# Expert rows fetched and added batch by batch inside the attention that follows, its first context loaded ahead of the expert weights, and the 64 wide attention unrolled

## The chip, the cores and the metric

The kernel runs as one program on one core of a Trainium2 chip. Its time is the device time of one execution in microseconds. The kernel before took 2455.58 us (median of three runs, 2454.81 to 2457.07). A core has five engines with instruction streams of their own: TensorE (PE: matmuls and transposes, with weight loads shown as PEld), VectorE (DVE), ScalarE (ACT), GpSimd (POOL) and SyncE (SP), which here only issues transfers. Engines meet through semaphores: an instruction adds to one when it is done, another engine waits for a value. Each stream is in order, so what stands behind a waiting instruction waits too.

## The reference

An input x (8 batches, 256 rows, 256 columns, float32) goes through eight gated branches, each `x = x + tanh(gate) * branch(layernorm(x))`, with a context of 8 x 256 x 192:

- layer 0: a cosine similarity with the context, then a feed-forward with one expert;
- layer 1: attention of 16 heads of width 16 on the context (l1x), then a mixture of 8 experts of 682 hidden columns, of which each row uses the two with the largest gate (l1f);
- layer 2: attention of 16 heads of width 64 on the context (l2x), then a mixture of 8 experts of 256 hidden columns, top 2, and two shared experts (l2f);
- layer 3: attention of 16 heads of width 16 on the context (l3x), then a self attention of width 16 with register rows (l3f).

```python
# layer 1 and 2, the mixtures, cut
top_v, top_i = top_k(gate_logits, 2)
out[row] = sum over the two chosen experts e of gate[row, e] * W3[e] @ (silu(W1[e] @ x[row]) * (W2[e] @ x[row]))
```

## The kernel before

x lies in SBUF through all branches as `x[128, 16, 256]`: 16 tiles of 128 rows, two tiles (T = 2) to each of the B = 8 batches. The branches run one after the other. At the end of each, DVE adds one to the semaphore `phase`, and the engines that touch shared buffers wait for it before they go on.

**Mixtures (l1f, l2f).** The 2048 rows are sorted by expert through a table in DRAM, `rows_by_expert`. POOL writes every row twice into it, at the slots of its two experts (line 835, an indirect DMA with the slots in `sli`). For 23 blocks of 256 rows, SP loads the block, PE transposes it and runs the up and down matmuls with weights split in high and low parts, ACT copies the result out, and SP stores it in place in the table (line 561, semaphores `ys0` to `ys3`). When every block has been stored, POOL fetches the rows back: for each of the 16 tiles two indirect DMAs of 128 rows (lines 851 to 855), 32 in all, into `r.back`, which lies over the arena from its start. DVE waits for eight at a time and then adds `gw * row` to x, two `scalar_tensor_tensor` instructions per tile, each followed by a wait for itself (lines 1390 to 1394). Only then does it raise `phase` (line 1398). `ch.link` is this wait of DVE for its own last instruction.

**The 64 wide attention (l2x)** follows l1f. For each batch n: DVE takes the mean and variance (`statistics`), POOL the power -0.5 (`root`, line 719), DVE writes the normed rows (`front`), PE transposes them, ACT copies them to `xt`. PE projects queries and keys (line 1877) and values (line 1890), which needs `xt`, the context `ct` and the weights. For each of 16 heads: scores (line 1900), maximum on DVE (line 1053), exponential on ACT (line 1555), on POOL one over the sum (line 889) and the multiplication by it (line 893), transposes on PE (line 1913), a copy on DVE (line 1062), values on PE (line 1928). After the heads, PE multiplies by the output weights (line 1958) and DVE adds to x (`finish`, lines 1075 and 954). The order is written out by hand: the statistics of batch n + 1 stand on DVE in the heads of batch n, after the copy of head 0 (`h == LAG`, line 1063), and its `root` stands on POOL after the multiplication of head 0 (line 895), before that of head 1. Batches 0 to 6 are one hardware loop on DVE, ACT, PE and POOL (`Fori(0, B - 1)`), batch 7 is written out behind it. SP loads contexts in `contexts` (line 491). Ahead of that, it issues ten transfers with the weights of the first five experts of l2f (`first_experts`, line 520), which wait for the same `phase` as the attention; they share its queue.

**The attention of l3x** follows l2f and is written out batch by batch. Its program (`packing`, one function on each engine) runs from n = -3 to B: in step n, PE makes the scores of batch n + 1 (line 2051, with the maxima on DVE, line 1133), those of batch n transposed (line 2065, exponential on ACT, line 1625, `clamp` on POOL, line 780) and its values (line 2085), and projects queries, keys and values of batch n + 3 (lines 1774 to 1776). POOL splits contexts (`context`), normed rows (`xT`), queries (`qhl`) and keys (`khl`) into two parts each (lines 750 and 752), adds a bias to x (line 773) and does the root. SP moves the split queries and keys into packed tiles (line 582). Before step -3, POOL sets three `kpack` tiles (line 738), a tile `qx` (lines 740 and 745) and does the root of batch 0; `with_bias(0)` comes last.

Of the kernel before, what the change touches and what calls it, by code (L numbers as in the profile page):

```python
# [13 lines left out]
F32 = mybir.dt.float32  # L14
# [8 lines left out]
P = 128  # L23
# [93 lines left out]
class Mix:  # L117
# [4 lines left out]
    def __init__(self, name, f, ring, cuts, slots, shared):  # L122
# [11 lines left out]
        self.total = {"lg": B, "gd": 1, "ga": 1, "rk": 1, "mk": 1, "sl": 1, "dy": 1, "sc": 16 * 2 * NT,  # L134
# [5 lines left out]
        for q in range(4):  # L140
            self.total[f"gt{q}"] = 16 * 2 * NT // 4
# [81 lines left out]
def build(nc, a, out, layers=8):  # L223
    ctx = ExitStack()
    with ctx:
# [42 lines left out]
        with ExitStack() as packed:  # L268
# [5 lines left out]
            oT16 = lay("oT16", [P, 4, S], F32)  # L274
            wqs16 = lay("wqs16", [P, 2, DC, D])
# [102 lines left out]
        for s in (L1F, L2F):  # L378
# [11 lines left out]
            r.back = arena[:, 0:2 * NT * D].rearrange("p (t d) -> p t d", d=D)  # L390
# [52 lines left out]
        mo = group("mo", "lg", "gd", "ga", "rk", "mk", "sl", "dy", "sc", "gt0", "gt1", "gt2", "gt3",  # L443
# [40 lines left out]
        def _(sp):  # L484
# [6 lines left out]
            def contexts(name, sem_in, sem_used, per):  # L491
# [151 lines left out]
        def _(pool):  # L643
# [89 lines left out]
            def packing(s):  # L733
                m, at = pk, s.base
                pool.wait_ge(g["phase"], n_phase[s.name] - 1)
                if not s.own:
                    for b in range(3):
                        nc.gpsimd.memset(kpack[b][:, :, :].bitcast(F32), 1.0).then_inc(m["ones"], 1)
                if s is L3X:
                    nc.gpsimd.memset(qx[:, :].bitcast(F32), 0.0).then_inc(m["qi"], 1)  # L740
                    pool.wait_ge(m["qi"], 1)
                    for j in range(2):
# [4 lines left out]
                        pool.wait_ge(m["qi"], 2 + j)  # L747

# [63 lines left out]
            def mixture(s):  # L812
# [38 lines left out]
                for t in range(NT):  # L851
                    for w in range(2):
                        nc.gpsimd.indirect_dma_start(  # L853
                            r.back[:, 2 * t + w, :], None, all_rows,
                            bass.IndirectOffsetOnAxis(ap=sli[:, w, t:t + 1], axis=0)).then_inc(m[f"gt{t // 4}"], 16)
                if not s.shared:
                    for dst, src in later:
                        pool.dma_start(dst, src).then_inc(g["w3_in"], 16)

            for name in run:  # L860
# [21 lines left out]
                else:  # L882
# [1511 lines left out]
```

## Time and profile before

| what | value |
|---|---|
| median of three runs | 2455.58 us |
| the profiled execution | 2458.67 us |
| its span in the trace | 2456.9 us |
| PE busy | 1932.6 us, 79% |
| DVE busy | 1015.9 us, 41% |
| ACT busy | 732.9 us, 30% |
| POOL busy | 999.5 us, 41% |
| granted TensorE clock, mean | 0.854 of 2.4 GHz |

Times in the trace count from the start of the span. A "busy" engine is one that executes an instruction other than a wait, a branch or the issue of a transfer; for POOL the issue of an indirect DMA is counted. The profile follows the chain of work that ended last back from the end; its shares say what lay on the path. A row of a timeline gives the start, the duration and in brackets the idle time of that engine before it, with what ended it. The stages lie in the span about so: l1f from 483 to 953 us, l2x to 1583, l2f to 1883, l3x to 2122.

### The profile page before, as it was taken

The page shows a single profiled execution, that of the slowest core. Times are in us where ns is not written, and L with a number is a line of the kernel's source. Part 1 is how long each engine was busy: PE and PEld are TensorE (multiplying, and loading weights), DVE is VectorE, ACT ScalarE, POOL GpSimd, SP SyncE. Part 2 cuts the span into 40 slices and gives each one's busy share as a digit, 9 for nine tenths or more (in the row PEclk, how much of TensorE's full clock was granted, in tenths as well). Part 3 has the DMA queues.
Part 4 walks back from the last instruction along what each step waited for, and adds up shares of the span by engine and source line. Part 5 has one row for each costly group of instructions (what it writes and reads, how often), then busy time and mean ns, then how long its engine had stood idle before and what let it go on. Part 6 is the DMA issues. An engine that isn't in the chain of part 4 may idle for free.

```text
span 2456.9 us, 33526 instructions
## 1 busy us (share of the span) xinstructions
PE 1932.6 (79%) x11738; PEld 1465.6 (60%) x11738; DVE 1015.9 (41%) x2339; ACT 732.9 (30%) x1721; POOL 999.5 (41%) x1044
## 2 busy tenths in 40 slices
PE   3589599727999962898988989769981899647997
PEld 2477466426888852555655656569970666435664
DVE  2434478531222212433334323543223578443773
ACT  1122056302222210332333323312330355312564
POOL 4010443064666643432344323461666676303320
PEclk9799789558999985888988989879995689766999
DMA  4270446114565543000000000012752645004441
GB/s 141 96 259 0 61 75 99 56 65 149 186 200 187 199 149 124 4 3 3 3 0 3 3 3 0 1 54 65 248 165 68 88 67 76 2 0 67 77 72 40
DMA packets 123393, 194.15 MB, mean 79 GB/s; under 512 B 12128, under 2 KB 99168, under 8 KB 122560
## 3 DMA queue, kind: packets, MB, share of 16 engines
q1 hardware_dynamic: 94288, 144.84, 24.6%
q0 software_dynamic: 8480, 26.65, 3.4%
q10 hardware_dynamic: 20496, 20.97, 2.6%
q8 instruction: 77, 1.26, 0.2%
q14 instruction: 52, 0.43, 0.1%
HBM read 109.84 MB, written 43.52 MB: 62 GB/s over the span
## 4 chain that ended last, share of the span: by engine, by line
PE 61%; issue 15%; POOL 9%; DVE 8%; DMA 3%; SPq 2%; ACT 2%; DVEq 0%; POOLq 0%; ACTq 0%
PE bank L2264 8%; PE bank L1774 6%; PE bank L2051 5%; PE bank L1900 5%; PE bank L1775 5%; PE bank L1776 5%; PE bank L1877 5%; PE bank L2085 3%; PE bank L1913 3%; PE bank L1928 3%; POOL arena L853 2%; PE bank L1890 2%; DVE nmf L1133 2%; SPq L582 1%; POOL rows_by_expert L835 1%
## 5 line engine op out<-in xcount | busy, mean ns | idle before, releaser
L1133 DVE TENSOR_REDUCE nmf<-bank 128x2 f32<-128x512 f32 x384 | 257.4, 688 | 144.8 <-PE bank L2051 142.9
L1625 ACT ACTIVATE pT<-bank 128x512 f32<-128x512 f32 x384 | 225.5, 595 | 224.2 <-PE bank L2065 222.7
L1774 PE MATMUL bank<-split,ewl 128*128 128x256 f32 x818 | 245.3, 300 | 9.6 <-DVE split L1361 9.6
L1371 DVE TENSOR_TENSOR arena<-sil,bank 128x256 f32<-128x256 f32 x216 | 91.1, 422 | 358.9 <-ACT sil L1709 358.8
L1776 PE MATMUL bank<-split,ewh 128*128 128x256 f32 x818 | 233.2, 285 | 0.0
L1775 PE MATMUL bank<-split,ewh 128*128 128x256 f32 x818 | 233.1, 285 | 0.0
L2051 PE MATMUL bank<-kpack,qpack 48*128 48x256 f32 (+1 forms) x768 | 199.6, 361 | 33.1 <-DVE nmf L1133 18.9
L889 POOL TENSOR_TENSOR esum<-esum,minus 128x2 f32<-128x2 f32 x128 | 89.2, 697 | 324.4 <-ACT arena L1555 324.2
L1489 ACT ACTIVATE arena<-bank 128x512 f32<-128x512 f32 x162 | 96.7, 597 | 388.4 <-PE bank L2264 158.5
L2264 PE MATMUL bank<-ew,arena 128*128 128x256 f32 (+1 forms) x864 | 210.2, 389 | 2.1 <-issue 2.1
L823 POOL TENSOR_TENSOR ewl<-ew,ewh 128x1536 fp32r<-128x1536 f32 (+1 forms) x71 | 206.9, 2914 | 5.7
L2065 PE MATMUL bank<-qpack,kpack 50*128 50x256 f32 (+1 forms) x768 | 192.8, 351 | 4.4 <-ACT pT L1625 4.1
L2051 PEld LDWEIGHTS bank<-kpack,qpack 48*128 48x128 f32 (+1 forms) x768 | 125.0, 213 | 118.6 <-DVE nmf L1133 57.1
L1555 ACT ACTIVATE arena<-bank,nmax 128x256 f32<-128x256 f32 x256 | 118.7, 469 | 244.1 <-DVE nmax L1053 242.1
L1053 DVE TENSOR_REDUCE nmax<-bank 128x2 f32<-128x512 f32 x128 | 87.6, 690 | 230.1 <-PE bank L1900 226.9
L2264 PEld LDWEIGHTS bank<-ew,arena 128*128 128x128 f32 (+1 forms) x864 | 155.2, 190 | 41.9 <-issue 25.3
L821 POOL CAST ewh<-ew 128x1536 fp32r<-128x1536 f32 (+1 forms) x71 | 88.4, 1245 | 212.4 <-DMA ew<-in_we 201.5
L1774 PEld LDWEIGHTS bank<-split,ewl 128*128 128x128 f32 x818 | 158.3, 194 | 18.4 <-issue 17.7
L1775 PEld LDWEIGHTS bank<-split,ewh 128*128 128x128 f32 x818 | 158.5, 194 | 0.8
L1900 PE MATMUL bank<-arena 64*128 64x256 f32 x512 | 154.0, 443 | 6.2 <-ACT arena L1489 6.2
L1776 PEld LDWEIGHTS bank<-split,ewh 128*128 128x128 f32 x818 | 158.3, 194 | 0.0
L1709 ACT ACTIVATE sil<-bank 128x256 f32<-128x256 f32 x216 | 82.7, 383 | 233.9 <-PE bank L1776 233.9
(403 smaller groups left out, 3844.1 us busy)
## 6 DMA issues: line engine op xcount, KB each, us to landing
ew<-in_we SPq DMA_DIRECT2D x46, 768.0 KB, 4.5
rows_by_expert<-mrow ACTq DMA_DIRECT2D x1, 20480.0 KB, 62.8
qpack<-qhl SPq DMA_DIRECT2D x144, 128.0 KB
kpack<-khl SPq DMA_DIRECT2D x144, 128.0 KB
ew<-in_we SPq DMA_DIRECT2D x23, 640.0 KB, 5.5
ew<-in_we SPq DMA_DIRECT2D x25, 512.0 KB, 4.4
arena<-rows_by_expert SPq DMA_DIRECT2D x46, 256.0 KB, 3.8
rows_by_expert<-arena SPq DMA_DIRECT2D x46, 256.0 KB, 4.1
```

Of the source, the lines that this page charges most:

```text
L823: nc.gpsimd.tensor_tensor(low, whole, high, ALU.subtract).then_inc(m["ws"], 1)
L1133: V.tensor_reduce(nmf[:, c, :, j, r], bank[h % 2][:, :].rearrange("p (t k) -> p t k", t=T), AXX, ALU.max, negate=True).then_inc(m["mx"], 1)
L1555: ins = A(prob[h % 3][:, t * S:(t + 1) * S], bank[h % 3][:, t * S:(t + 1) * S], ACT.Exp, bias=nmax[:, h, t:t + 1], accum_out=esum[:, h, t: ...
L1625: A(pT16[i % 8][:, :], bank[2 + h % 2][:, :], ACT.Exp, scale=s.qscale).then_inc(m["e"], 1)
L1774: mm(out_, al, bh, start=start, stop=False)
L1775: mm(out_, ah, bl, start=False, stop=False)
L1776: return mm(out_, ah, bh, start=False, stop=stop)
L1877: ins = mm(dst, w[:, c, gr * P:(gr + 1) * P], of[:, c, :], start=c == 0, stop=c == kt_ - 1)
L1900: ins = mm(bank[h % 3][:, t * S:(t + 1) * S], qT[r0:r0 + 64, gr, t * P:(t + 1) * P], kT[r0:r0 + 64, gr, :], start=True, stop=True)
L2051: ins = mm(bank[h % 2][:, t * S:(t + 1) * S], q[rows, r, t * P:(t + 1) * P], k[rows, r, :], start=True, stop=True)
L2065: ins = mm(bank[2 + h % 2][:, t * S:(t + 1) * S], k[rows, r, t * P:(t + 1) * P], q[rows, r, :], start=True, stop=True)
L2264: ins = mm(bank[4 + k % 2][:, q * D:(q + 1) * D], r.hid[(s.a0[k] + n) % s.slots][rr, q * P:(q + 1) * P], expert_down(s, w)[rr, h, :], star ...
```

## The change

1. The 32 indirect fetches and the additions leave the end of both mixtures. POOL's part ends when every block is stored, DVE waits for the same (`ys0` to `ys3`) and raises `phase`.
2. A new function `gather(s, n)` on POOL issues the four indirect DMAs of batch n, into one of three buffers. A new function `add_rows(ch, s, n)` on DVE waits for these four, does the four additions with two links (tile 0 and 1 of the first expert, link, tile 0 and 1 of the second, link), and adds one to `ga`; the fetch of batch n from n = 3 on waits for the additions of batch n - 3.
3. In l2x POOL issues the fetches of batches 0 and 1 before its first root, and those of batch n + 2 after the last head of batch n. DVE adds batch 0 before `statistics(0)`, batch n + 1 at `h == LAG` in the heads of batch n, directly before `statistics(n + 1)`.
4. In l3x POOL sets `qx` first, then issues the fetches of batches 0 and 1, then sets the `kpack` tiles; the fetch of batch n + 5 stands at the head of step n (n = -3 to 2), before `context`. DVE adds batch 0 before `statistics(0)` and batch n + 4 at `h == 8` of step n.
5. SP issues the first context of l2x ahead of the ten transfers of expert weights.
6. The loops over batches 0 to 6 of l2x are written out on DVE, ACT, PE and POOL.
7. The three transfers of l3x weights (`later`) go from the end of l1f to the end of l2x on POOL, since the fetch buffers of l1f lie over their target.

```diff
@@ SP
                 sp.dma_start(ct[:, :, :], a["ctxT"][0, :, :, :]).then_inc(sem_in, 16)
+                if sets:
+                    first_experts(sets, a["we2"])
...
-            if "l2f" in run:
-                first_experts(L2F, a["we2"])
             if "l2x" in run:
-                contexts("l2x", ph["l2x"]["ct"], ph["l2x"]["v"], L2X.vjobs)
+                contexts("l2x", ph["l2x"]["ct"], ph["l2x"]["v"], L2X.vjobs, L2F if "l2f" in run else None)
@@ POOL, packing
                 pool.wait_ge(g["phase"], n_phase[s.name] - 1)
-                if not s.own:
-                    for b in range(3):
-                        nc.gpsimd.memset(kpack[b][:, :, :].bitcast(F32), 1.0).then_inc(m["ones"], 1)
                 if s is L3X:
...
+                    for n in range(2):
+                        gather(L2F, n)
+                if not s.own:
+                    for b in range(3):
+                        nc.gpsimd.memset(kpack[b][:, :, :].bitcast(F32), 1.0).then_inc(m["ones"], 1)
...
                     ahead = 0 <= n + 3 < B
+                    if s is L3X and 2 <= n + 5 < B:
+                        gather(L2F, n + 5)
@@ POOL, mixture
                     pool.wait_ge(m[f"ys{q}"], at[f"ys{q}"] + s.total[f"ys{q}"])
-                for t in range(NT):
+
+            all_rows = table.rearrange("b s d -> (b s) d")
+
+            def gather(s, n):
+
+                m, at = mo, s.base
+                if n >= 3:
+                    pool.wait_ge(m["ga"], at["ga"] + n - 2)
+                for t in range(T):
                     for w in range(2):
                         nc.gpsimd.indirect_dma_start(
-                            r.back[:, 2 * t + w, :], None, all_rows,
-                            bass.IndirectOffsetOnAxis(ap=sli[:, w, t:t + 1], axis=0)).then_inc(m[f"gt{t // 4}"], 16)
-                if not s.shared:
-                    for dst, src in later:
-                        pool.dma_start(dst, src).then_inc(g["w3_in"], 16)
+                            rooms[s.name].back[n % 3][:, w, t, :], None, all_rows,
+                            bass.IndirectOffsetOnAxis(ap=sli[:, w, n * T + t:n * T + t + 1], axis=0))\
+                            .then_inc(m[f"gt{n % 3}"], 16)
@@ POOL, l2x
+                    gather(L1F, 0)
+                    gather(L1F, 1)
                     root(m, 1, rstd[:, :], rstd[:, :], mhalf[:, 0:T])
-                    with pool.Fori(0, B - 1) as n:
-                        normalise(n, True)
-                    normalise(B - 1, False)
+                    for n in range(B):
+                        normalise(n, n < B - 1)
+                        if n + 2 < B:
+                            gather(L1F, n + 2)
+                    pool.wait_ge(mo["ga"], L1F.base["ga"] + B)
+                    for dst, src in later:
+                        pool.dma_start(dst, src).then_inc(g["w3_in"], 16)
@@ DVE
+            def add_rows(ch, s, n):
+
+                m, at = mo, s.base
+                dve.wait_ge(m[f"gt{n % 3}"], at[f"gt{n % 3}"] + 16 * 2 * T * (n // 3 + 1))
+                for w in range(2):
+                    for t in range(T):
+                        r = n * T + t
+                        ins = stt(x[:, r, :], rooms[s.name].back[n % 3][:, w, t, :], gw[:, w, r:r + 1], x[:, r, :],
+                                  ALU.mult, ALU.add)
+                    ch.link(ins)
+                V.memset(idle[:, 0:1], 0.0).then_inc(m["ga"], 1)
...
                         if h == LAG and ahead:
+                            add_rows(ch, L1F, n + 1)
                             statistics(n + 1)
...
+                add_rows(ch, L1F, 0)
                 statistics(0)
...
-                with dve.Fori(0, B - 1) as n:
-                    ch.loop(n, 2 * T + LN)
+                for n in range(B - 1):
                     heads(n, True)
                     projected(n + 1)
                     heads(n + 1, False, range(LAG))
                     finish(n)
-                ch.leave(B - 1)
@@ DVE, packing
+                    if s is L3X:
+                        add_rows(ch, L2F, 0)
                     statistics(0)
...
+                        if h == 8 and n + 4 < B and s is L3X:
+                            add_rows(ch, L2F, n + 4)
                         if h == 10 and n + 4 < B and not s.own:
                             statistics(n + 4)
@@ DVE, mixture
-                for t in range(NT):
-                    if t % 4 == 0:
-                        dve.wait_ge(m[f"gt{t // 4}"], at[f"gt{t // 4}"] + 16 * 8)
-                    for w in range(2):
-                        ch.link(stt(x[:, t, :], r.back[:, 2 * t + w, :], gw[:, w, t:t + 1], x[:, t, :], ALU.mult, ALU.add))
+                for q in range(4):
+                    dve.wait_ge(m[f"ys{q}"], at[f"ys{q}"] + s.total[f"ys{q}"])
@@ ACT and PE, l2x
-                with act.Fori(0, B - 1) as n:
+                for n in range(B - 1):
...
-                with pe.Fori(0, B - 1) as n:
+                for n in range(B - 1):
```

## Rows read from the trace of the kernel before

**Rows 1.** The page, the chain that ended last: shares by engine.
```profile
PE 61%; issue 15%; POOL 9%; DVE 8%; DMA 3%; SPq 2%; ACT 2%; DVEq 0%; POOLq 0%; ACTq 0%
```
**Rows 2.** The chain in order of time, 903 to 984 us: start, us, what.
```profile
903.55 2.13 DMA rows_by_expert<-arena
...
906.61 1.03 POOL arena L853
...
946.37 2.72 DMA arena<-rows_by_expert,sli
...
958.47 8.97 DMA ct<-in_ctxT
...
967.57 15.69 PE bank L1877 x64
```
**Rows 3.** Timelines of POOL, DVE and ACT, 915 to 958 us.
```profile
915.52 0.96 POOL L853 DMA_INDIRECT arena<-rows_by_expert,sli  x1 [0.31 <-issue]
...
918.29 4.17 DVE L1394 SCALAR_TENSOR_TENSOR x<-arena,gw,x 128x256 f32<-128x256 f32 x8 [21.65 <-DMA arena<-rows_by_expert,sli]
...
954.69 0.72 POOL L719 TENSOR_TENSOR rstd<-rstd,mhalf 128x2 f32<-128x2 f32 x1 [5.69 <-DVE rstd L1030]
...
957.45 0.60 ACT L1489 ACTIVATE xt<-bank 128x512 f32<-128x512 f32 x1 [54.07 <-PE bank L1860]
```
**Rows 4.** Timelines of POOL, PE and DVE in l2x: batch 1's heads, and batch 7's (last row).
```profile
1073.34 0.69 POOL L719 TENSOR_TENSOR rstd<-rstd,mhalf 128x2 f32<-128x2 f32 x1 [8.74 <-DVE rstd L1030]
...
1075.87 1.11 PE L1913 MATMUL bank<-ident,arena 128*128 128x128 f32 x4 [4.34 <-POOL arena L893]
...
1070.83 0.69 DVE L1053 TENSOR_REDUCE nmax<-bank 128x2 f32<-128x512 f32 x1 [0.52 <-DVE x L954]
...
1537.03 0.69 DVE L1053 TENSOR_REDUCE nmax<-bank 128x2 f32<-128x512 f32 x1 [0.20 <-DVE x L954]
```
**Rows 5.** Stretches, one per batch of l2x: us, busy (instructions) by engine, PE clock, DMA.
```profile
1272.51:1350.92 78.41, 69.52 (x308) 46.21 (x309) 27.62 (x49) 23.64 (x77) 28.22 (x33) 0.89 0.01 3
1350.92:1424.64 73.72, 64.82 (x308) 43.61 (x309) 27.34 (x49) 23.53 (x77) 28.12 (x33) 0.95 0.01 3
```
**Rows 6.** The chain in order of time, 1833 to 1901 us.
```profile
1833.95 2.13 DMA rows_by_expert<-arena
...
1883.68 5.32 POOL kpack L738 x3
...
1890.55 0.73 POOL rstd L719
...
1900.72 0.58 PE bank L1774
```
**Rows 7.** Timelines of POOL and PE, start of l3x.
```profile
1921.83 0.61 POOL L750 CAST khl<-kf 128x512 fp32r<-128x512 f32 x1 [0.82 <-DMA kpack<-khl]
...
1928.87 0.58 PE L1774 MATMUL bank<-xT,rows 128*128 128x256 f32 x1 [0.43 <-POOL xT L752]
```
**Rows 8.** POOL's clamp of head 3 and the values on PE, steps 0 and 2.
```profile
1944.99 0.61 POOL L750 CAST cT<-ct 96x512 fp32r<-96x512 f32 x1 [1.54 <-PE bank L1776]
...
1949.17 0.61 POOL L780 TENSOR_SCALAR pT<-pT 128x512 f32<-128x512 f32 x1 [0.48 <-ACT pT L1625]
...
2002.13 0.61 POOL L780 TENSOR_SCALAR pT<-pT 128x512 f32<-128x512 f32 x1 [0.36 <-ACT pT L1625]
...
1950.62 1.84 PE bank L2085 x16
...
2003.20 0.99 PE bank L2085 x16
```
**Rows 9.** DVE timeline in l3x: two instructions beside POOL, one with POOL idle.
```profile
1891.31 0.73 DVE L1128 TENSOR_SCALAR xn<-x,mv,rstd 128x256 f32<-128x256 f32 x2 [5.80 <-POOL rstd L719]
...
1907.33 1.95 DVE L1128 TENSOR_SCALAR xn<-x,mv,rstd 128x256 f32<-128x256 f32 x2 [10.42 <-POOL rstd L719]
...
2010.09 0.69 DVE L1133 TENSOR_REDUCE nmf<-bank 128x2 f32<-128x512 f32 x1 [0.48 <-PE bank L2051]
```

More of the change, by code:

```diff
@@ L133, in __init__ @@
         self.base = defaultdict(int)
-        self.total = {"lg": B, "gd": 1, "ga": 1, "rk": 1, "mk": 1, "sl": 1, "dy": 1, "sc": 16 * 2 * NT,
+        self.total = {"lg": B, "gd": 1, "gx": 1, "rk": 1, "mk": 1, "sl": 1, "dy": 1, "sc": 16 * 2 * NT,
                       "wh": self.parts * self.sets, "ws": self.parts * self.sets,
@@ L139, in __init__ @@
             self.total[n] = self.a0[-1]
-        for q in range(4):
-            self.total[f"gt{q}"] = 16 * 2 * NT // 4
+        self.total["ga"] = B
+        for q in range(3):
+            self.total[f"gt{q}"] = 16 * 2 * T * len(range(q, B, 3))
         for q in range(4):
@@ L274, in build @@
             oT16 = lay("oT16", [P, 4, S], F32)
+            with nc.sbuf_tensor("back16", [P, 3 * 2 * T * D], F32) as back16:
+                pass
             wqs16 = lay("wqs16", [P, 2, DC, D])
@@ L389, in build @@
             assert o[0] <= ARENA, (o[0], ARENA)
-            r.back = arena[:, 0:2 * NT * D].rearrange("p (t d) -> p t d", d=D)
+            r.back = [(back16 if s.shared else w13)[:, k * 2 * T * D:(k + 1) * 2 * T * D].rearrange("p (w t d) -> p w t d", w=2, t=T)
+                      for k in range(3)]
         assert o[0] <= ARENA, (o[0], ARENA)
@@ L442, in build @@
         l0f = group("l0f", "yc", "h", "hc", "y", "dve")
-        mo = group("mo", "lg", "gd", "ga", "rk", "mk", "sl", "dy", "sc", "gt0", "gt1", "gt2", "gt3",
+        mo = group("mo", "lg", "gd", "gx", "rk", "mk", "sl", "dy", "sc", "gt0", "gt1", "gt2", "ga",
                    "w0", "w1", "w2", "w3", "w4", "wd0", "wd1", "wd2", "wd3", "wd4", "wh", "ws", "xg0", "xg1", "xg2", "xg3",
@@ L489, in _, with contexts @@
                 sp.dma_start(dst, src).then_inc(g["w0_in"], 16)
-            def contexts(name, sem_in, sem_used, per):
+            def contexts(name, sem_in, sem_used, per, sets=None):
                 if n_phase[name] > 1:
@@ L1063, in heads @@
                         if h == LAG and ahead:
+                            add_rows(ch, L1F, n + 1)
                             statistics(n + 1)
-                        if isinstance(n, int) and n == B - 1 and 0 <= h - 4 < B - 1 and not steps_:
+                        if n == B - 1 and 0 <= h - 4 < B - 1 and not steps_:
                             stats_of(h - 4)
@@ L1275, in mixture @@
                 if s.shared:
-                    dve.wait_ge(m["ga"], at["ga"] + 1)
+                    dve.wait_ge(m["gx"], at["gx"] + 1)
                     ch.link(V.tensor_reduce(gm[:, :], sel[:, :, :], AXX, ALU.add))
@@ L1299, in mixture @@
                 if not s.shared:
-                    dve.wait_ge(m["ga"], at["ga"] + 1)
+                    dve.wait_ge(m["gx"], at["gx"] + 1)
                 ch.link(tt(sel[:, :, :], sel[:, :, :], lg[:, :, :], ALU.mult))
@@ L1557, in heads @@
                             ins.then_inc(m["e"], 1)
-                        if h == FRONT + 1 and not isinstance(n, int):
+                        if h == FRONT + 1 and n < B - 1:
                             front(n + 1)
@@ L1696, in mixture @@
                 act.wait_ge(m["gd"], at["gd"] + 1)
-                A(sel[:, :, :], sel[:, :, :], ACT.Exp).then_inc(m["ga"], 1)
+                A(sel[:, :, :], sel[:, :, :], ACT.Exp).then_inc(m["gx"], 1)
                 def high_part(k):
@@ L1878, in project @@
                             ins.then_inc(m[what], 1)
-                    if isinstance(n, int):
+                    if n == 0:
                         pe.wait_ge(g["w2b_in"], 16 * 2)
```

## The prediction

> **What bounds the kernel now.** I read the page's chain of waits first, then the same chain in order of time at the two places where a mixture ends, then the timelines of each engine there and in the stages behind it, and last the stretches of l2x. PE carries 61% of the chain [rows 1]; what matters is where it does not. At the end of l1f the table is stored at 905.7 us. POOL then issues 32 indirect DMAs, the first at 906.61, the last at 946.37, so one each 1.28 us; the last lands after 2.72 us [rows 2]. DVE adds in pace with them, eight additions in 4.17 us, 0.52 us each, the last eight done at 953.3 [rows 3]. Statistics follow; POOL's root starts at 954.69 and the transposed rows are in `xt` at 958.05 [rows 3]. But PE starts the projections only at 967.57, since the first context, issued at 958.47 behind ten weight transfers, takes 8.97 us to land [rows 2]. From the stored table to the first projection: 61.9 us. At the end of l2f the store lands at 1836.08; memsets of `kpack` start at 1883.68 and take 5.32 us, the root of batch 0 starts at 1890.55, the first projection at 1900.72 [rows 6]. Both stretches are latency with PE idle, so what leaves them is gained in full, and what is put on the chain of the next stage is paid in full.
>
> **Start of l2x.** The fetches of batches 0 and 1 stay ahead: the eighth starts at 915.52 as today, 1.27 us apiece, and ends at 916.48 [rows 3]; the root follows at about 916.7. DVE beside it: fetch 4 starts at 906.61 + 3 x 1.27 = 910.4, lands 2.72 us later at 913.1, four additions of 0.52 and 1.3 us of statistics (953.35 to 954.6) end at 916.5. Both paths meet at 916.7. From the root to `xt` it is 3.4 us (954.69 to 958.05) [rows 3], so the projections could start at 920.3, 47.3 us earlier. Against it: 3.9 MB of expert weights are now in flight at just that time. Today nothing runs beside the fetches; the nearest row is the context behind these weights, 8.97 us instead of 2.4 [rows 2]. A fetch has a queue of its own, so it need not wait for all of them. Its landing is bounded by 2.72 and by 8.97 us; I take twice 2.72 in round numbers, 2.9 us more. That leaves 44.4 us (bounds 41 and 47).
>
> The first context ahead of the weights is worth 9.4 us today (958.05 to 967.57, less the issue), but nothing in the new order: behind the weights it would be there 14 us after the phase (953.4 to 967.4), at about 920, before `xt` is. I count it within the 44.4 and not again.
>
> **Additions in l2x, seven times.** In batch n POOL has multiplied head 0 and stands in the root of batch n + 1, which waited 8.74 us for DVE's `rstd`; heads 1 and on stand behind it on POOL, and PE waits 4.34 us for them [rows 4]. So the statistics are on the chain in every batch, with nothing beside. The four additions stand directly before them: 4 x 0.52 = 2.1 us, seven times, +14.6 us. Bounds: 11 (two of a pair overlap a little) and 17. The fetches themselves (5.1 us a batch) start after POOL's last head, while PE projects and multiplies by the output weights; POOL is idle there for some 28 us, so they cost nothing; without this cover each batch would pay 5.1.
>
> **Unrolling.** At the head of each looped batch DVE loses 0.52 us before its first maximum where the unrolled batch 7 loses 0.20 [rows 4]. With about as much (0.17) on ACT at the tail of the batch, 7 x 0.49 = -3.4 us (bounds 0 and -6). The Trainium skill (Runtime: NRT & Kernel Launch, Instruction fetch mechanics) says that instructions stream in ahead in order and that a taken branch can force a fetch; by it each of seven back edges could hold such a fetch, and writing them out would bring more than I count. The trace shows only the 0.3 us, and the sum goes by that.
>
> **Clock.** After the wait of 4.34 us PE runs at 1.2 GHz, in most batches for some 13 us. A batch takes 78.41 us at a mean granted clock of 0.89, but 73.72 us where it came back earlier (0.95) [rows 5]. With a wait of 6.4 us I expect the slow kind to stay the rule. One batch more or less of either kind is 4.7 us: it goes into the range, at zero in the sum. The transfers of l3x weights at the end of l2x fall into POOL's idle time: zero.
>
> l2x together: -44.4 + 14.6 - 3.4 = **-33.2 us**.
>
> **Start of l3x.** The phase comes at about 1836.3. `qx` takes 1.6 us, eight fetches 10.2 (to 1848.4), `kpack` 5.3, the root starts at 1853.9 instead of 1890.55 [rows 6]: -36.7 us. DVE is there earlier (fetch 4 lands at 1845, additions and statistics end at 1848.6) and hides behind POOL. But then three times four fetches stand at the head of steps -3, -2 and -1, each 4 x 1.27 = 5.1 us, ahead of the context, of `xT`, `qhl` and `khl`. POOL is what the start of l3x waits for: the gaps between its work are 0.82 us (its `khl` waits for packed keys) and PE waits for its `xT` [rows 7]. So 3 x 5.1 - 0.8 = +14.4.
>
> **Fetches in steps 0, 1, 2.** There POOL's clamps of heads 0 to 3 must be done before PE's values. In step 0 POOL had 1.54 and 0.48 us to wait on the way and the clamp ended 0.84 us before PE came: 5.1 - 2.9 = 2.2 us. In step 2 it had 0.36 and ended 0.46 before: 5.1 - 0.8 = 4.3 [rows 8]. Step 1 I put between them, 3.2. Sum +9.7 (bounds 0 and 15.3).
>
> **Additions in steps -1 to 3** (those of -3 and -2 hide behind POOL). Four take 2.1 us alone. DVE has about 0.48 us of idle time before a maximum, and PE can run one head ahead [rows 9]. But DVE also suffers beside POOL: the same pair of instructions took 1.95 us beside POOL's work where it took 0.73 alone, 0.6 more for one [rows 9]. Four additions are thus between 2.1 and 4.5 us, less a slack of some 1 us: I take 2.0 for each step, five times, +10 (bounds 0 and 22). On this stands a rule of the Trainium skill (SBUF — State Buffer, "SBUF: two separate sides"): a DVE instruction with two inputs in SBUF and a GpSimd instruction exclude each other for their whole length. The long row agrees. By it the additions, with two such inputs, go at the upper end in l3x and at 2.1 in l2x, where POOL waits.
>
> l3x together: -36.7 + 14.4 + 9.7 + 10 = **-2.6 us**. l1f, l2f and all else are as before. Sum: **-35.8 us**. The profiled execution took 2458.67 us with a span of 2456.9, so 1.8 lie around the span and stay; it would be 2422.9. It stands 3.1 above the median of the runs; from the median 2455.58 the same difference gives **2420 us**.
>
> **Rivals.**
> 1. *The fetches and additions hide in l3x.* For it: DVE and POOL are not busy all the time there, and PE at 1.2 GHz leaves slack. Against it: rows 7 and 8 show POOL ahead of PE by less than a microsecond. Then l3x brings -36.7 + 14.4 + 4 = -18, l2x -36: 2401 us. 23%.
> 2. *POOL and DVE exclude each other fully in l3x*, the skill's rule above. The five additions go at 4.4 less nothing, +22, the fetches at +15.3: l3x -36.7 + 14.4 + 15.3 + 22 = +15; l2x with landings at 8.97 and 17 us of additions: -41 + 17 - 2 = -26: 2445 us. For it the long row [rows 9]; against it that DVE is not beside POOL at all times. 15%.
> 3. *Slower: the unrolled l2x has its instructions late.* A body of about 310 matmuls and as many weight loads is then fetched seven times by PE instead of once. It would take 36 / 7 = 5.1 us of stall in each batch to eat the gain, beyond that it is slower; at 6 us a batch 2462 us. Against it: batch 7 of l2x and all of l3x are written out already and show no such wait. 4%.
> 4. *It does not do what it says*: the attention waits for the last fetch after all, through POOL's order or one of the three buffers (`ga`). Then 32 fetches still stand before l2x and l3x; the context's 9.4 us, the unrolling's 3.4 and two additions of 2.1 are gained, 14.6 in l2x and some 2 in l3x are added: about 2455 us, no change. Against it: every wait on `ga` is for additions two steps back. 3%.
>
> **Numbers.** Forecast 2420 us, 55%, its own range 2408 to 2434. With rivals 1 and 2 the range is 2398 to 2440, which leaves out their far parts and rival 3. Two kernels closer than 0.2% (4.9 us) can't be told apart here. Faster by more than that: 0.93; within it: 0.03, rival 4; slower: 0.04, rival 3.
>
> **What would show it.** The first `xt` projection of l2x 15 to 19 us after the last store of l1f; if it is at 25, the weights slow the fetches. PE's wait before head 1 at 6.4 us in seven batches; if it stays at 4.3, the additions are hidden. Batches of l2x at 80 us. The root of batch 0 of l3x 17.8 us after the store, the first values of l3x (1950.62 now) about 20 us earlier, and its last ones only about 3. DVE's additions longer than 0.52 us in l3x and not in l2x. The prediction is wrong if l3x as a whole gains over 12 or loses over 10 us, or if the batches of l2x come out under 77 us.

## The result, and the profile after

The changed kernel took 2391.14 us (median of 4, 2380.09 to 2392.55), the kernel before beside it 2455.19 us (median of 4): a ratio of 0.9731, 95% interval 0.970 to 0.9763. The forecast was 2420 us with a range of 2398 to 2440, so the direction was right and the gain was larger than the range allows. Measured once more in another session (z1_same_again below), the same kernel had a ratio of 0.9805 (0.9772 to 0.9838) and 2406.78 us. The two intervals don't overlap, though no instruction differs, and most of what follows is about that difference.

The stages, each between two marks of the profile: the start of the last store of a mixture, PE's first projection of l2x, the end of PE's last output matmul of l2x, the start of DVE's last addition to `x` of l3x, the end. All in us; the last column is what the prediction gave for the difference of the first two. The prediction counted from the landing of the store, 2.13 us after its start: its 15 to 19 us to the first projection came out at 17.2, its 17.8 us to the first root of l3x at 17.6.

| stretch | before | after | z1 (same code) | after - before | forecast |
|---|---|---|---|---|---|
| start to last store of l1f | 903.6 | 906.9 | 903.1 | +3.4 | 0 |
| that store to first projection | 64.0 | 19.4 | 19.7 | -44.6 | -44.4 |
| l2x | 613.1 | 597.1 | 615.4 | -16.0 | +11.2 |
| to last store of l2f | 253.3 | 249.0 | 247.9 | -4.3 | 0 |
| that store to end of l3x | 298.0 | 295.6 | 293.1 | -2.4 | -2.6 |
| l3f | 325.0 | 322.2 | 322.7 | -2.8 | 0 |
| span | 2456.9 | 2390.2 | 2401.9 | -66.7 | -35.8 |

The start of l2x came out within 0.2 us of the forecast. So did l3x, but that is luck, since its profiles scatter by 10 us (below). Three stages that nothing touched scatter by 3 to 4 us, and l2x is off by 27.

The start of l2x in the changed kernel, from the chain of waits in order of time (start, us, what), answers to [rows 2, 3]:

```profile
913.87 5.85 DMA w<-rows_by_expert,sli
...
919.74 0.89 DVE x L1045 x2
...
922.90 0.74 POOL rstd L723
...
926.31 2.07 PE bank L1910 x4
```

The fourth fetch, issued at 913.87, takes 5.85 us to land, where the last fetch of the kernel before took 2.72; the additions, the statistics and the root hang on it.

One batch of l2x in the changed kernel: timelines of DVE, POOL and PE around head 1 (the answer to [rows 4]):

```profile
1103.97 0.42 DVE L1108 TENSOR_TENSOR scr<-bank,bo_l2x 128x256 f32<-128x256 f32 x1 [5.86 <-PE bank L1991]
...
1107.14 1.79 DVE L1045 SCALAR_TENSOR_TENSOR x<-w,gw,x 128x256 f32<-128x256 f32 x4
...
1110.28 0.70 POOL L723 TENSOR_TENSOR rstd<-rstd,mhalf 128x2 f32<-128x2 f32 x1 [9.80 <-DVE rstd L1062]
...
1112.81 1.11 PE L1946 MATMUL bank<-ident,arena 128*128 128x128 f32 x4 [5.48 <-POOL arena L907]
1113.86 2.07 PE L1933 MATMUL bank<-arena 64*128 64x256 f32 x4
...
1118.81 1.29 PE L1933 MATMUL bank<-arena 64*128 64x256 f32 x4
...
1120.62 1.13 PE L1933 MATMUL bank<-arena 64*128 64x256 f32 x4
```

The additions take 1.79 us and lie on the path as forecast, PE waits 5.48 us instead of 4.34. Then a group of four score matmuls takes 2.07 us (1.2 GHz), but already 6 us later 1.13 again (2.4 GHz). In the kernel before the low clock lasted some 17 us in most batches (an estimate from 78.4 us at a mean of 0.89). The stretches from one root to the next, two of the changed kernel (us, busy time and count for PE, PE loads, DVE, ACT, POOL; granted clock; DMA share; GB/s), answer to [rows 5]:

```profile
1035.25:1110.28 75.03, 65.16 (x308) 43.74 (x308) 28.78 (x55) 23.52 (x77) 32.08 (x37) 0.93 0.04 10
...
1335.51:1410.60 75.09, 65.22 (x308) 43.80 (x308) 28.77 (x55) 23.52 (x77) 32.08 (x38) 0.93 0.04 10
```

PE's busy time is 65.2 us a batch where the slow kind of the kernel before has 69.5, with a matmul count that is the same: PE did the same work at another clock.

Over the whole of l2x PE executes 2460 matmuls in each kernel, so its time splits into idle time, which the waits make, and busy time, which differs with the clock. Four stretches in the same columns: the kernel before, the changed one, and z1_same_again and y1_early_stats, which come below:

```profile
967.57:1580.67 613.10, 544.91 (x2460) 363.74 (x2460) 220.64 (x393) 189.44 (x616) 224.83 (x263) 0.91 0.01 2
...
926.31:1523.40 597.09, 521.92 (x2460) 350.88 (x2460) 229.31 (x428) 188.87 (x616) 249.93 (x290) 0.93 0.03 9
...
922.80:1538.20 615.40, 540.22 (x2460) 361.95 (x2460) 230.71 (x428) 189.44 (x616) 250.37 (x290) 0.91 0.03 9
...
928.03:1473.18 545.15, 503.10 (x2460) 340.77 (x2460) 229.42 (x428) 188.99 (x616) 251.57 (x290) 0.99 0.04 10
```

From before to after PE's idle time rose by 7.0 us (68.2 to 75.2) and its busy time fell by 23.0 (544.9 to 521.9): together the -16.0 of the table. The forecast had +11.2 for the waits and nothing for the clock.

### The profile page after: what moved, and what is told of

Its sections match the earlier page's. It is cut to its first block, busy times and chain, and to the rows that moved or that the text cites. A ratio compares the mean times of both kernels' runs of the same rounds, so it can differ in the third digit from the quotient of the medians.

```text
span 2390.2 us, 32787 instructions
## 1 busy us (share of the span) xinstructions
PE 1915.6 (80%) x11738; PEld 1456.2 (61%) x11738; DVE 1015.2 (42%) x2355; ACT 732.4 (31%) x1721; POOL 1001.4 (42%) x1044
## 4 chain that ended last, share of the span: by engine, by line
PE 64%; issue 13%; DVE 10%; POOL 7%; ACT 2%; DMA 2%; SPq 1%; DVEq 0%; POOLq 0%; ACTq 0%
PE bank L2297 8%; PE bank L1807 6%; PE bank L2084 5%; PE bank L1808 5%; PE bank L1809 5%; PE bank L1933 5%; PE bank L1910 5%; PE bank L2118 4%; PE bank L1946 3%; PE bank L1961 3%; PE bank L1991 2%; PE bank L1923 2%; DVE nmf L1165 2%; POOL rows_by_expert L843 1%; PE bank L2145 1%
## 5 line engine op out<-in xcount | busy, mean ns | idle before, releaser
L1522 ACT ACTIVATE arena<-bank 128x512 f32<-128x512 f32 x162 | 96.7, 597 | 375.9 <-PE bank L2297 157.3
L1807 PEld LDWEIGHTS bank<-split,ewl 128*128 128x128 f32 x818 | 159.1, 195 | 18.4 <-issue 17.6
L1933 PE MATMUL bank<-arena 64*128 64x256 f32 x512 | 143.8, 420 | 6.2 <-ACT arena L1522 6.2
```

The lines of the kernel that those rows point to most:

```text
L1807: mm(out_, al, bh, start=start, stop=False)
L1933: ins = mm(bank[h % 3][:, t * S:(t + 1) * S], qT[r0:r0 + 64, gr, t * P:(t + 1) * P], kT[r0:r0 + 64, gr, :], start=True, stop=True)
```

## What made l2x shorter

Three theories. A: writing the batches out shortens them. B: the longer wait before head 1 makes the clock come back sooner. C: the clock repeats one of several patterns from batch to batch, and which one is not decided by the instructions; C was put up only after the first two rounds of kernels. Four kernels on one chip came first. In the code cuts a remark behind `#` is the author's and does not stand in the kernel.

**x1_written**: the kernel before, with the l2x loops written out on all four engines.

```diff
-                with pe.Fori(0, B - 1) as n:
+                for n in range(B - 1):
                     heads(n, True)
...
```

> The kernel before with only the eight batches of l2x written out on PE, ACT, DVE and POOL; the 32 fetches and the additions stay where they are before l2x and l3x. Theory A (it is the writing out that shortens the stretch at 1.2 GHz): batches 1 to 6 at 73 us instead of 77.9 on the mean (75.1 of the changed kernel less 1.8 of additions), the whole at 2455 - 27 = about 2428 us. Theory B (it is the longer wait of PE that ends the low clock sooner): the wait before head 1 is 4.0 us, the batches stay at 77.5, the whole is 2452. My own term of the prediction was -3.4 us.

**x2_written_pause**: that kernel with four more DVE instructions in each batch. **x3_looped_pause** has the same four instructions in the loops of the kernel before.

```diff
                         if h == LAG and ahead:
+                            stand_in(n + 1)      # 2 x T stt of x into scr
                             statistics(n + 1)
```

> The kernel of x1_written with four DVE instructions more before the statistics of each next batch (same form and length as the additions, their output is read by nothing), so that only the wait of PE before head 1 grows by 1.8 us to about 5.5. Theory A: the batches are 1.8 us longer than in x1_written, 75.1, the whole 13 us above x1_written. Theory B: the batches go from 77.5 to 75.1, the whole about 15 us below x1_written, near 2438.

> The kernel before, still looped, with the same four DVE instructions more in each batch. Their output is read by nothing. Theory A: 7 x 1.8 = 12.6 us slower, 2468, low clock for 15 us in each batch as before. Theory B: PE's wait goes from 4.34 to 6.1 us and the low clock ends sooner, batches at 75.5, the whole 2440.

**x4_early_adds**: the changed kernel, its additions a step earlier.

```diff
                         if h == LAG and ahead:
-                            add_rows(ch, L1F, n + 1)
                             statistics(n + 1)
...
                     projected(n + 1)
                     heads(n + 1, False, range(LAG))
+                    if n + 2 < B:
+                        add_rows(ch, L1F, n + 2)
                     finish(n)
```

> The changed kernel with the four additions of l2x's batch n+2 moved ahead of DVE's last step of batch n, where DVE is idle for 5.9 us; the statistics stay. PE's wait before head 1 should go from 5.48 to about 3.7 us. Theory A: the batches lose these 1.8 us, 75.1 to 73.3, the whole 2391 - 12 = 2379. Theory B: the short wait brings the long stretch at 1.2 GHz back, batches at 77.5, the whole 2391 + 15 = 2406.

Measured, against the kernel before on the same chip (2457.91 us); the wait is that of the second batch on, shorter by 1.2 to 1.8 us in the first:

| kernel | median us | ratio, 95% | wait before head 1 | batches of l2x | l2x |
|---|---|---|---|---|---|
| x1_written | 2435.97 | 0.9903 (0.9867 to 0.9939) | 3.65 | 77.0 and 72.9 in turn | 597.7 |
| x2_written_pause | 2434.48 | 0.9911 (0.9886 to 0.9937) | 5.48 | 74.7 to 75.1 | 595.8 |
| x3_looped_pause | 2455.38 | 1.0004 (0.9973 to 1.0035) | 6.15 | 76.1 and 77.3 in turn | 608.2 |
| x4_early_adds | 2392.48 | 0.9742 (0.9698 to 0.9786) | 3.65 | 73.1 and 77.2 in turn | 595.4 |

Neither A nor B gives all of this; x2 alone came near B, which had 2438 us for it. The profiled execution of x1 was its slowest (2453.02 us): it lost time in l1f (911.3 us) and l3x (307.6), so only its l2x is read here. Two stretches of x1_written, the same instructions one batch apart:

```profile
1155.94:1232.98 77.04, 69.02 (x308) 45.92 (x308) 27.29 (x50) 23.66 (x77) 28.20 (x33) 0.89 0.01 3
1232.98:1305.97 72.99, 64.96 (x308) 43.61 (x308) 27.02 (x50) 23.56 (x77) 28.12 (x33) 0.95 0.01 3
```

With the same wait of 3.65 us before each, one has PE busy for 69.0 us and the next for 65.0. Four instructions on the path (x2 against x1) cost 1.84 us seven times in waits: PE's idle time in l2x rose by 12.9 us (62.3 to 75.2), its busy time fell by 14.8 (535.5 to 520.7), and l2x became 1.9 us shorter. In x3 against the kernel before it was +12.8 and -17.7, 613.1 to 608.2. Taking the additions off the path (x4 against the changed kernel) was -12.6 and +10.9, and brought 1.7 us. The clock gave back or took about what the wait changed: the last two of these batches together took 150.1 or 150.2 us in x1, x2, x4 and the changed kernel alike, at waits of 3.65 and of 5.49 us.

**y1_early_stats** takes away the wait itself; the kernels y2 and y3, made for l3x, run l2x as the changed kernel has it.

```diff
+                        add_rows(ch, L1F, n + 2)
+                        statistics(n + 2)
                     finish(n)
...
                         if h == LAG and ahead:
-                            add_rows(ch, L1F, n + 1)
-                            statistics(n + 1)
```

> The changed kernel with additions and statistics of l2x's batch n+2 both moved ahead of DVE's last step of batch n, where DVE is idle for 5.9 us. POOL's root then has its input before POOL reaches it, so PE's wait before head 1 should fall from 5.48 us to about 1. Theory B (the wait is what brings the low clock): hardly any stretch at 1.2 GHz is left, batches at about 69.5 us as the last batch ran at 0.98 to 1.00, the whole 2391 - 7 x 5.5 = about 2353 us. Rival (the low clock comes by itself, the wait only moves where it falls): the low stretches stay at 7 to 10 us a batch, batches at 73 to 75, the whole 2380 to 2390.

2369.92 us, ratio 0.9529 (0.9485 to 0.9572). Two stretches of its l2x, and the root of its batch:

```profile
1089.85:1157.15 67.30, 62.27 (x309) 42.23 (x308) 28.77 (x54) 23.52 (x77) 32.32 (x38) 1.00 0.04 11
1157.15:1224.46 67.31, 62.28 (x310) 42.23 (x308) 28.78 (x54) 23.53 (x77) 32.30 (x37) 1.00 0.04 12
```

```profile
1022.55 0.70 POOL L723 TENSOR_TENSOR rstd<-rstd,mhalf 128x2 f32<-128x2 f32 x1 [0.46 <-DVE rstd L1062]
```

POOL waits 0.46 us for DVE, not 9.80; PE's longest wait in a batch is 0.9 us, and the clock stays at 2.4 GHz in every batch but the first. So the long wait is what brings the low clock at all, and a batch without both takes 67.30 us: l2x 545.2 us, where the expectation had 69.5 for a batch. The 75.09 us of the changed kernel are these 67.30, 4.84 more of PE's idle time (9.87 against 5.03) and 2.95 more of its busy time (65.22 against 62.27). Over all of l2x y1 has 33.1 us less idle and 18.8 us less busy time.

In the same session y2 and y3 had l2x at 618.4 and 618.6 us, with batches of 78.5 to 79.2, after a wait of 5.49 us to the hundredth. That is theory C, and it was tested next.

**z1_same_again** is the changed kernel with no edit. **z2_late_start** has the four extra DVE instructions once, before the first statistics of l2x. **z3_double_adds** has them in every batch, behind the additions.

```diff
                 add_rows(ch, L1F, 0)
+                later_(0)                        # z2: once
...
                             add_rows(ch, L1F, n + 1)
+                            again(n + 1)         # z3: in each batch
                             statistics(n + 1)
```

> The changed kernel once more, nothing edited. In y2 and y3 the same l2x code with the same wait of 5.49 us before head 1 ran its batches at 78.5 us and 0.89 of the clock, where the first profile of the changed kernel had 75.09 and 0.93. Theory C (two repeating patterns of the clock, and the instructions do not decide which): the batches are all near 75.1 or all near 78.5, the difference 21 us over l2x, with nothing in between; on the chip of y2 the whole is then near 2424 us or, relative to the kernel before, 0.973. Theory B (the wait decides): always 75.1.

> The changed kernel with four DVE instructions of 0.45 us more once, ahead of the first statistics of l2x; what they write is read by nothing. The projections start 1.8 us later, all later instructions are the same. If the start of l2x relative to the clock's changes picks the pattern (theory C), its batches may come out at the other of the two values, the whole 21 us away from z1_same_again; otherwise the whole is 1.8 us longer.

> The changed kernel with four more instructions like the additions in each batch of l2x, between these and the statistics; what they write is read by nothing. PE's wait before head 1 goes from 5.49 to 7.3 us. By the sum of the prediction each such set costs its own length: 7 x 1.8 = 12.6 us more than z1_same_again. If the clock's pattern absorbs or doubles it, the batches are 67.3 + 7.3 and 2.3 or 5.9 for the low stretch, 76.9 or 80.5 us, and the whole is between -9 and +35 us of z1_same_again.

| kernel | median us (6 runs) | ratio, 95% | wait before head 1 | batches of l2x | l2x |
|---|---|---|---|---|---|
| z1_same_again | 2406.78 | 0.9805 (0.9772 to 0.9838) | 5.49 | 79.3 to 78.6, the last 75.4 | 615.4 |
| z2_late_start | 2393.16 | 0.9744 (0.9709 to 0.978) | 5.49 | 74.9 to 75.1 | 596.9 |
| z3_double_adds | 2423.34 | 0.9849 (0.9812 to 0.9885) | 7.33 | 76.7 to 81.2, mixed | 624.7 |

z1, the timeline of PE and two stretches, to be laid beside those of the same code above:

```profile
1116.48 1.11 PE L1946 MATMUL bank<-ident,arena 128*128 128x128 f32 x4 [5.49 <-POOL arena L907]
1117.52 2.07 PE L1933 MATMUL bank<-arena 64*128 64x256 f32 x4
...
1125.52 2.07 PE L1933 MATMUL bank<-arena 64*128 64x256 f32 x4
...
1131.05 1.13 PE L1933 MATMUL bank<-arena 64*128 64x256 f32 x4
```

```profile
1192.67:1271.28 78.61, 68.74 (x308) 45.99 (x308) 29.05 (x55) 23.64 (x77) 32.17 (x38) 0.89 0.03 10
...
1349.85:1425.24 75.39, 65.53 (x308) 44.06 (x308) 28.77 (x55) 23.53 (x77) 32.07 (x37) 0.93 0.03 10
```

Same kernel, same wait, and the score matmuls still take 2.07 us nine microseconds after it; PE is busy for 68.7 us instead of 65.2. C holds: profiles of the changed l2x code, with nothing in l2x edited, came out near 597 us three times (the first one, z2 with its late start, q1 below) and at 615 to 619 us five times (y2, y3, z1, and q2 and q3 below), and never between. A batch is the 67.3 us of y1, 4.8 us more of idle time, and 3.0 or 6.5 us more of busy time. It is not one kind for every batch, as the last stretch of z1 shows (75.39). The chip alone doesn't decide it either: z1 and z2 ran on one chip, and so did q1, q2 and q3. z2 began l2x 1.8 us later and had the other pattern than z1, in its profile; its six runs lie at 2382.6 to 2401.0, those of z1 at 2401.5 to 2415.1. That fits a pattern picked by when l2x starts, but a single shift doesn't prove it. What picks it stays open. Twice the additions (z3) cost 9.3 us against z1 (12.8 more of idle, 3.5 less of busy time) and 27.6 against the first profile, where their own length is 12.9: the number depends on which pattern one compares with.

## The other terms

**y2_spread_fetches** moves the fetches of l3x into POOL's wait for the queries; **y3_l3x_ahead** puts all 32 fetches and additions of the second mixture ahead of l3x again.

```diff
-                    if s is L3X and 2 <= n + 5 < B:
-                        gather(L2F, n + 5)
...
                             parts(xT16, xt[:, :, :], "xs", n + 3)
+                        if s is L3X and 2 <= n + 5 < B and 4 <= h < 8:
+                            gather(L2F, n + 5, (h - 4,))
```

```diff
-                    for n in range(2):
+                    for n in range(B):                # y3, POOL, ahead of kpack
                         gather(L2F, n)
...
-                        add_rows(ch, L2F, 0)
+                        for n in range(B):            # y3, DVE, ahead of statistics(0)
+                            add_rows(ch, L2F, n)
```

> The changed kernel with the fetches of l3x's steps moved from the head of a step (four in a row) to behind the split of xT, one before each of heads 4 to 7. My terms of the prediction (fetches in steps -3 to -1 cost 14.4, in steps 0 to 2 9.7 us): POOL waits 3.9 to 5.0 us for the queries there, so the steps -3 to -1 come 3 x 3.9 = 11.7 us earlier, and in steps 0 to 2 some 5 us more are won; l3x 17 us shorter, 2375 in all. Rival (these fetches were never what l3x waited for, PE and its clock were): within 5 us of 2391.

> The changed kernel with all 32 fetches and all additions of the second mixture ahead of l3x again, as the kernel before has them; l2x is that of the change. By my prediction l3x as a whole gained only 2.6 us from the change: 2394 us, the first root of l3x 31 us later. Rival 1 of the prediction (the fetches hide, l3x gained 18 us): 2409. That l3x lost by the change: below 2386.

The kernel before took 2491.29 us in that session, so only ratios are used: 0.9694 (0.9651 to 0.9737) for y2, 0.9759 (0.9691 to 0.9827) for y3; the times expected were for a session like the first. From the last store of l2f, in the profiles:

| kernel | first root | first values on PE | l3x |
|---|---|---|---|
| before | 56.6 | 116.6 | 298.0 |
| after | 19.7 | 96.9 | 295.6 |
| y2_spread_fetches | 19.7 | 83.2 | 281.0 |
| y3_l3x_ahead | 50.8 | 110.7 | 293.7 |
| q3_no_l3x_adds | 19.7 | 96.7 | 286.6 |

Timelines of POOL, first of the changed kernel, then of y2_spread_fetches:

```profile
1806.11 1.26 POOL L758 TENSOR_TENSOR xT<-xt,xT 128x512 fp32r<-128x512 f32 x1
1811.30 0.61 POOL L756 CAST qhl<-qf 128x512 fp32r<-128x512 f32 x1 [3.92 <-ACT qf L1631]
```

```profile
1844.90 1.26 POOL L758 TENSOR_TENSOR xT<-xt,xT 128x512 fp32r<-128x512 f32 x1
1846.33 1.04 POOL L871 DMA_INDIRECT back<-rows_by_expert,sli  x1 [0.17 <-issue]
...
1850.18 0.95 POOL L871 DMA_INDIRECT back<-rows_by_expert,sli  x1 [0.30 <-issue]
1851.14 0.62 POOL L756 CAST qhl<-qf 128x512 fp32r<-128x512 f32 x1
```

At the head of a step the four fetches delay everything, and POOL then idles 3.92 us for the queries; behind `xT` they fill that idle time. First values 13.7 us earlier: the 14.4 that the prediction charged to steps -3 to -1 were real, and avoidable. l3x as a whole was 15.3 us below the mean of the kernels that follow (17 expected); in y4 and z4, with the same edit, it took 286.0 and 278.1 us. l3x in the profiles of the changed code without an edit to it, that of the changed kernel among them, scatters from 290.7 to 301.2 us (mean of eight 296.3), and in the code before, over four profiles, from 296.6 to 307.6 (301.3); y3, with everything ahead of l3x again, lies within the first range at 293.7. That l3x gains little as a whole is shown; 2.4 and 5 us can't be told apart.

Three kernels, run once each, took one term away each. q3 leaves out the additions of seven batches.

```diff
                 if sets:
+                    sp.wait_ge(ph[name]["q"], 1)     # q1
                     first_experts(sets, a["we2"])
...
-                sp.dma_start(ct[:, :, :], a["ctxT"][0, :, :, :]).then_inc(sem_in, 16)
                 if sets:
                     first_experts(sets, a["we2"])
+                sp.dma_start(ct[:, :, :], a["ctxT"][0, :, :, :]).then_inc(sem_in, 16)    # q2
...
                         if h == 8 and n + 4 < B and s is L3X:
-                            add_rows(ch, L2F, n + 4)
+                            dve.wait_ge(...)          # q3: add_rows' wait and signal alone
+                            V.memset(idle[:, 0:1], 0.0).then_inc(mo["ga"], 1)
```

> The changed kernel with the ten weight transfers of the second mixture held back until PE has done its first projection of l2x, so that nothing is in flight beside the first fetches. By my guess of 2.9 us for these transfers the fourth fetch lands 2.7 us after its start instead of 5.9, and the first projection comes 16.5 us after the last store of l1f instead of 19.4 to 20.1. If POOL or DVE were the limit anyway: unchanged at 19.4 to 20.1.

> The changed kernel with the first context issued behind the ten weight transfers, as in the kernel before. By the prediction it is worth nothing in the new order: the context lands about 14 us after the phase, before xt is ready, so the first projection stays at 19.4 to 20.1 us after the last store. If the context is still late: above 22 us, and PE waits for ct.

> The changed kernel without the additions of the second mixture's rows for batches 1 to 7 in l3x, waits and signals kept (so its output leaves those rows out). By the prediction the additions cost 2 us in each of steps -1 to 3: the first values of l3x come about 2 us earlier than 96.9 us after the last store, and l3x is 10 us shorter than the 293 to 301 us of the other runs. If they hide: values at 96.9, l3x within 3 us of the mean 297. If POOL and DVE shut each other out fully: 20 us shorter.

**q1** (2386.26 us): the first projection 16.6 us after the last store of l1f, against 19.4. The weights beside the fetches cost 2.7 us: without them the first four fetches land after 2.7 to 2.9 us, as in the kernel before, where they took 5.6 to 6.4 beside them. In the chain of waits, POOL's own eight fetches are now what the root comes behind:

```profile
916.56 0.96 POOL w L870
...
917.55 0.75 POOL rstd L724
...
920.98 4.21 PE bank L1911 x9
```

**q2** (2405.41 us): 20.5 us. The context, issued behind the weights, lands 11.8 us after its issue and is the last thing waited for, about a microsecond late: next to nothing, as forecast. The time of q2 is 19 us above that of q1 for another reason: its l2x took 618.4 us, that of q1 596.5.

```profile
912.80 11.79 DMA ct<-in_ctxT
924.60 0.14 issue
924.74 5.32 PE bank L1910 x17
```

**q3** (2399.61 us): l3x 286.6 us, 9.7 below the mean of the others (forecast 10) and 4 below the lowest of them; the first values hardly move, so the cost falls in the later steps. One profile against a scatter of 10 us: the size is plausible, not shown. An addition beside a two-input instruction of POOL is long. DVE in the changed kernel, while POOL adds the bias (1816.10, 1.44 us):

```profile
1815.94 2.79 DVE L1045 SCALAR_TENSOR_TENSOR x<-back,gw,x 128x256 f32<-128x256 f32 x4
```

Three of the four take 0.48 us, one 1.48. That agrees with the rule of the Trainium skill (SBUF — State Buffer, "SBUF: two separate sides") for that one; beside POOL's fetches they stay at 0.48. The long row that the prediction built on [rows 9] is of an instruction with one tensor input (`x`; mean and root are one value per row), so it did not bear on the two inputs; this one does.

**The better version.** y4_both joins y1 and y2; z4_both_again is the same kernel beside z1.

> The changed kernel with the edits of y1_early_stats and y2_spread_fetches together. If both theories hold and the parts add: 2391 - 38 - 17 = 2336 us. If only the wait in l2x counts 2353, if only the fetches 2375.

> The kernel of y4_both once more beside the changed kernel on one chip. Without a wait before head 1 there is no low stretch in l2x and so no choice of pattern: batches 67.3 us, l2x 545 us as in y1 and y4, the whole 0.97 to 0.975 of z1_same_again. If y4 only met a good chip: above 0.985.

y4: 2358.71 us, ratio 0.9493 (0.9451 to 0.9535). z4: **2324.79 us**, ratio 0.9461 (0.9431 to 0.9492), 0.966 of z1 on the same chip, l2x 546.4, l3x 278.1; 0.970 to 0.975 was expected. It is faster than both kernels. The sum in y4's expectation took 38 us for l2x; it was 69 to 73 against the pattern of z1 and y2, and 52 against the first profile.

## Why the prediction was wrong

- **Start of l2x**, -44.4: measured -44.6, with the guess of 2.9 us for the traffic at 2.7 (q1). Right, and the context at nothing too (q2).
- **The step that failed is the clock**: "With a wait of 6.4 us I expect the slow kind to stay the rule. One batch more or less of either kind is 4.7 us: it goes into the range, at zero in the sum." Measured, this zero is -23.0 us, PE's busy time in l2x at the same matmuls; it is most of the 27.2 us by which l2x missed (597.1 where the sum had 624.3). The batches don't draw their kind one by one. They fall into a pattern: all six stretches of the changed kernel from root to root were 75 us. The other pattern (z1, y2, y3, q2, q3) took 615.4 to 618.6 us, with PE's busy time 4.7 us below that of the kernel before in z1; by the ratio of z1 the time would be 2407 us, inside the range. So the range reached one of two outcomes and left out the other. [Rows 5] held the warning: batches of equal code at 78.41 and 73.72. The prediction's own sign of being wrong, batches of l2x under 77 us, came true at 75.1.
- **Waits in l2x**, +11.2: PE's idle time rose by 7.0, the other 4.2 us of the miss. Of these terms the **additions**, +14.6, cost 12.9 in waits (1.84 us for four, x2 and z3). As time they are not a number: -1.9 (x2 against x1), -4.9 (x3 against before), +9.3 (z3 against z1).
- **Unrolling**, -3.4: PE's idle time fell by 5.9 us (x1), of which 4.0 are its wait before head 1 (4.31 to 3.65 in six batches; in the first it stayed at 2.48). l2x fell by 15.4, the other 9.5 being busy time, in a pattern in which only every second batch has the long low stretch. Nothing in it needs late or early instructions, so rival 3 has nothing for it. The Trainium skill's rule on fetch across a taken branch (Runtime: NRT & Kernel Launch, "Instruction fetch mechanics") isn't needed for the difference either. The traces settle it: from 1045 to 1540 us, while its loops turned, the kernel before moved nothing on its two instruction queues, and x1_written moved 31 packets on them over l2x, with PE's idle time shorter and not longer.
- **PE's wait** of 6.4 us: it was 5.49. The prediction added the additions to 4.34 and left out its own unrolling term, which took 0.66 off this wait, and it took the additions at 0.52 us each, where four of them took 1.79 to 1.84.
- **l3x**, -2.6: measured -2.4, root -36.9 against -36.7, first values -19.7 against about -20. The root and the first values are hits; that the whole agrees to 0.2 us is luck, as it scatters by 10 us. Rivals 1 and 2 needed -18 and +15 there and are out. The additions, +10, were near 9.7 in one profile (q3), but fell in the later steps: the first values, for which 2 us were charged, moved by 0.2. Rival 4 is out: the attention starts at the fourth fetch.
- **Stages nobody touched** brought -3.7 together, which is their scatter.

## What to carry to other kernels

Where a wait is long enough for PE's clock to fall, price the wait and the low clock together, for all repetitions at once: the batches of a regular loop settle into a pattern, all of one kind or two kinds in turn, and the same code can have either of two patterns. A forecast then has two centres, one per pattern, and the range has to reach both. The lever is the wait itself: move what hangs on it (here four additions and the statistics) into idle time a step earlier, and both the wait and the low clock go.

## What the runs showed of the hardware

- The same instructions with the same wait of 5.49 us gave 597 or 615 to 619 us for a stage, by the clock alone. Where PE's longest wait in a batch was 0.9 us (y1) the clock stayed up.
- An indirect fetch landed after 5.85 us beside ten weight transfers of 3.9 MB in all and after 2.72 without them (q1), and the context issued behind these after 11.79.
- In the session of y1 to y4, l2f took 274 to 277 us in all four profiles, where all others have 247 to 253. The timeline of ACT in y1_early_stats:

```profile
1536.50 0.38 ACT L1744 ACTIVATE sil<-bank 128x256 f32<-128x256 f32 x1 [6.73 <-remote]
1551.98 0.38 ACT L1744 ACTIVATE sil<-bank 128x256 f32<-128x256 f32 x1 [15.10 <-remote]
```

It waits for something on a queue that the profile doesn't name, while POOL's indirect stores run. The kernel before was slower in that session too, by 34 us (2491 against 2457). No profile of it was kept there, so it is not shown that the same stage slowed it, and the ratios of that session rest on its having done so; z4_both_again, in a session without it (l2f 249 us), has about the ratio of y4_both (0.9461 and 0.9493). The cause isn't known.
